# The hand-over from a window graph block to a two-way ConvLSTM scan: a new order of row blocks, and scan step 0 directly behind the last gather

## The reference, cut to what matters

```python
# layer 0: x is (16, 48, 32, 32)
y = affine(conv1x1(x, fc1_w, fc1_b), fc1_s, fc1_t)
nodes = windows of 8x8 pixels, 64 nodes of 48 channels each
idx = knn_idx(nodes, 9)                       # by normalized distance
feat = concat([x_i, x_j - x_i]); h = gelu(affine(feat @ ew + eb)); h = max over the 9 neighbours
x1 = affine(conv1x1(h, fc2_w, fc2_b), fc2_s, fc2_t) + x
...
# layer 1: rows of x1 are the time steps of a ConvLSTM, forward and backward
def step(carry, xr):                          # xr: (B, C, W), one image row
    h, c = carry
    gates = conv1d(concat([xr, h]), w_mid, width 3) + b
    i, f, g, o = split(gates, 4)
    c2 = sigmoid(f) * c + sigmoid(i) * tanh(g)
    h2 = sigmoid(o) * tanh(c2)
    return (h2, c2), h2
hs_f = scan(step, x1 rows 0..31); hs_b = scan(step, x1 rows 31..0)
y = w_proj @ concat([hs_f, hs_b]); y = relu(batchnorm(y)) + x1
```

## Time and profile before

| | us |
|---|---|
| median of 3 runs | 713.08 (711.72 to 713.14) |
| profiled execution, own time | 711.41 |
| span of the profiled execution | 709.5 |
| PE / DVE / ACT / POOL busy | 594.8 / 547.1 / 469.0 / 121.0 |
| mean granted PE clock | 0.94 |

### The profile page before, as it was taken

The page is one execution under the profiler, slowest core; times in us unless marked ns, Lnnn a source line. Parts: engine busy times, 40 slices in busy tenths (PEclk is TensorE's granted clock), DMA queues, the critical chain, the costliest instruction groups (busy, mean ns, idle before and its releaser), DMA issues.

```text
span 709.5 us, 12789 instructions
## 1 busy us (share of the span) xinstructions
PE 594.8 (84%) x3380; PEld 340.0 (48%) x3380; DVE 547.1 (77%) x1035; ACT 469.0 (66%) x675; POOL 121.0 (17%) x106
## 2 busy tenths in 40 slices
PE   5966799999999999987847888888889999988930
PEld 1213555555555555544414555555555555545500
DVE  1678799999999999993883777777777778767745
ACT  3631488888888888883852666666666666756635
POOL 2620122222222222233546000000000000000000
PEclk9987799999999999996987999999999999999965
DMA  8847755655655656686312111111111222276216
GB/s 221 256 130 194 187 121 132 130 132 131 134 133 131 135 130 132 134 154 141 73 18 56 44 45 44 45 45 45 41 30 52 69 74 72 55 155 152 77 55 177
DMA packets 98621, 75.99 MB, mean 107 GB/s; under 512 B 51765, under 2 KB 80951, under 8 KB 97879
## 3 DMA queue, kind: packets, MB, share of 16 engines
q1 hardware_dynamic: 97830, 72.06, 43.6%
q10 hardware_dynamic: 768, 3.67, 2.1%
HBM read 48.74 MB, written 22.35 MB: 100 GB/s over the span
## 4 chain that ended last, share of the span: by engine, by line
PE 45%; ACT 17%; DVE 13%; issue 13%; DMA 7%; SPq 3%; ACTq 1%; DVEq 1%
PE pz L602 13%; PE pz L695 8%; PE pz L688 6%; PE p_out L610 4%; ACT he L882 3%; ACT tgo L873 3%; ACT gel L813 3%; DMA y_d<-y 3%; PE p_edge L563 3%; PE p_keys L550 2%; PE pz L674 2%; ACT selfg L807 2%; PE p_edge L565 2%; PE p_edge L706 2%; ACT tif L867 2%
## 5 line engine op out<-in xcount | busy, mean ns | idle before, releaser
L1140 DVE TENSOR_REDUCE hmax<-gel 96x128 f32<-96x1024 f32 x128 | 154.1, 1205 | 33.1 <-ACT gel L813 32.5
L813 ACT ACTIVATE gel<-pz 96x1024 f32<-96x1024 f32 x128 | 130.7, 1023 | 58.2 <-PE pz L602 56.7
L674 PE MATMUL pz<-xh,w_xh 128*112 (+1 forms) x384 | 102.9, 404 | 8.2 <-issue 8.2
L695 PE MATMUL pz<-ht,w_xh 128*112 128x512 f32 x384 | 107.1, 414 | 3.1 <-DMA ht<-xh 3.1
L877 ACT ACTIVATE tc<-c 48x512 f32<-48x512 f32 x64 | 40.2, 628 | 68.0 <-DVE c L1228 68.0
L674 PEld LDWEIGHTS pz<-xh,w_xh 128*112 128x112 f32 x384 | 68.0, 177 | 33.4 <-issue 9.5
L695 PEld LDWEIGHTS pz<-ht,w_xh 128*112 128x112 f32 x384 | 62.1, 175 | 44.0 <-issue 24.9
L1235 DVE SCALAR_TENSOR_TENSOR h<-tgo,tc 48x512 f32<-48x512 f32 x64 | 44.0, 688 | 49.3 <-ACT tc L877 49.3
L688 PE MATMUL pz<-ht,w_e 48*112 48x512 f32 x192 | 60.7, 423 | 23.6 <-ACT he L882 23.6
L1033 POOL TENSOR_TENSOR xh<-kl,xh 48x512 f32 (+1 forms) x32 | 38.6, 1208 | 175.3 <-DVE idx L1116 90.4
L1219 DVE SCALAR_TENSOR_TENSOR cu<-tif,c 48x512 f32<-48x512 f32 x64 | 44.1, 690 | 24.6 <-ACT tif L867 23.2
(11 more groups left out here) (114 smaller groups left out, 1021.3 us busy)
## 6 DMA issues: line engine op xcount, KB each, us to landing
ib<-idx_d SPq DMA_DIRECT2D x64, 256.0 KB, 4.4
y_d<-y SPq DMA_DIRECT2D x32, 192.0 KB, 3.4
y_hl<-y_d SPq DMA_DIRECT2D x32, 192.0 KB, 4.3
hist_d<-h SPq DMA_DIRECT2D x64, 96.0 KB, 1.9
hp<-hist_d SPq DMA_DIRECT2D x32, 192.0 KB, 2.7
kr<-xn_d SPq DMA_DIRECT2D x32, 98.0 KB
xn_d<-x_in SPq DMA_DIRECT2D x32, 96.0 KB, 2.2
kl<-xn_d SPq DMA_DIRECT2D x32, 96.0 KB
```

The costliest lines, as they stand in the source:

```text
L674: pe.matmul(pz[0:TOP, 2 * d + m, :], w_xh[:, 0, d, m, t], rhs, start=(t == 0), stop=False)
L695: mm = pe.matmul(pz[0:TOP, 2 * d + m, :], w_xh[:, 1, d, m, t], moving(ht, slice(0, P), t), start=False, stop=(t == TAPS - 1))
L813: act.activation(gel[:, t % 2], pz[0:O, 2 * (t % 2):2 * (t % 2) + 2, :], ACT.Gelu) \
L1140: dve.tensor_reduce(dst, gel[:, t % 2].rearrange("p w (r c k) -> p w r c k", r=WS, k=KN), AX_X, ALU.max).then_inc(S["maxed"], 1)
```

## The change

Row blocks are processed in order 0, 3, 2, 1, by a function `place` that turns a group number into row block and pair. After 16 groups the scan has the rows it needs for its first 8 steps in both directions. Scan step 0 waits on PE for `x1_split` 16, `wl_split` 2 and the gelu of the gather that used the same PSUM banks, and leaves out its L688 matmuls (h is zero). fc2 of the last group follows step 0 on PE, `fc2_out` and `x1_high` of it are placed inside ACT's steps 0 and 1, and step 1 waits for `wl_split` 3.

The scan weights are loaded two turns earlier, scaled by POOL one turn earlier, and split by DVE in turns 29, 30 and 31, in place of the `topk` calls that these turns don't have. The rests in the padding rows come out of a masked multiply-add (raw weight plus head times 0 or -1 per partition). The mask `rests` is set by a POOL memset, four transfers of one element per partition, and a POOL multiplication. The four transfers L390 and the tile `wl_rest` are gone. The padding rows of `x1r` are loaded by one more transfer per step 26 to 29, in place of POOL's memset. One more pair of turns (24, 25) is written out rather than looped.

```diff
-            wr, p = g // PAIRS, g % PAIRS
+            wr, p = place(g)
...
+        def place(g):
+            return g // PAIRS * 3 % WROWS, g % PAIRS
...
-            with engine.Fori(1, GROUPS // 2 - 3) as j:
+            with engine.Fori(1, GROUPS // 2 - 4) as j:
...
@@ SP, load_scan_weights @@
-                sp.wait_ge(S["wl_split"], 3)
-                for k, first, n in ((0, C, HALF - C), (0, TOP, P - TOP), (1, C + 1, 1), (1, TOP, P - TOP)):
-                    sp.dma_start(w_xh[first:first + n, k].bitcast(F32), wl_rest[...]).then_inc(S["wl_moved"], 16)
+                sp.wait_ge(S["rests_set"], 1)
+                for k, first, n in ((0, C, HALF - C), (0, TOP, P - TOP), (1, C + 1, HALF - C - 1), (1, TOP, P - TOP)):
+                    sp.dma_start(rests[first:first + n, k:k + 1], ones_sel[0:n, 0, 0:1],
+                                 allow_slow_non_contiguous=True).then_inc(S["rests_here"], 16)
...
@@ SP, turn @@
-                if isinstance(j, int) and nth(j, b, 0)[0] == GROUPS - 6:
+                if isinstance(j, int) and nth(j, b, 0)[0] == GROUPS - 8:
                     load_scan_weights()
-                if isinstance(j, int) and nth(j, b, 0)[0] == GROUPS - 2:
+                if isinstance(j, int) and nth(j, b, 0)[0] in (GROUPS - 4, GROUPS - 3):
+                    d = nth(j, b, 0)[0] - (GROUPS - 4)
+                    sp.wait_ge(S["x1_hi"], 2 * PAIRS)
+                    sp.wait_ge(S["pads_set"], 9)
                     for s in range(2):
-                        load_twins(s, 0, s)
-                    sp.wait_ge(S["pads_set"], 9)
-                    load_third(0, 0)
+                        load_twins(s, d, s)
+                    load_third(0, d)
...
@@ SP, behind the turns @@
-            move_scan_weights()
-            sp.wait_ge(S["x1_hi"], GROUPS)
-            (twins and third of direction 1; store_x1 of the last group; its waits; loads of wp, gb, comb)
             step(0, 0)
+            store_x1(GROUPS - 1, 1, GROUPS // 2 - 1)
+            step(1, 1)
+            (waits for all x1 stores and x1_split 32; loads of wp, gb, comb)
...
@@ SP, steps 26 to 29 @@
+                    sp.dma_start(x1r[C:HALF, reg(i, 0, 4)],
+                                 x1_d[reg(i, H // 2, 4), 0:HALF - C].rearrange("r c b w -> c r (b w)")) \
+                        .then_inc(S["x1r_loaded"], 16)
...
@@ PE @@
-            pe.wait_ge(S["gelus"], 4 * GROUPS)
-            pe.wait_ge(S["wl_split"], 4)
-            pe.wait_ge(S["wl_moved"], 64)
+            pe.wait_ge(S["x1_split"], 2 * PAIRS)
             pe.wait_ge(S["zeros_set"], 2)
+            pe.wait_ge(S["wl_split"], 2)
+            pe.wait_ge(S["gelus"], 4 * GROUPS - 1)
             x_part(0, 0, 0, 0)
             h_part(0, 0)
-            pe.wait_ge(S["x1_split"], GROUPS)
+            pe.wait_ge(S["gelus"], 4 * GROUPS)
             x_part(0, 1, 0, 0)
             h_part(0, 1)
             x_part(1, 0, 1, 0)
+            fc2(GROUPS - 1, 1, GROUPS // 2 - 1)
+            pe.wait_ge(S["wl_split"], 3)
...
@@ ACT, step @@
+                    if isinstance(s, int) and s == 0 and d == 1:
+                        fc2_out(GROUPS - 1, 1, GROUPS // 2 - 1)
                     tanh_cell(s, d)
                     if d == 0:
                         tanh_i_f(s, 1)
...
+                    if isinstance(s, int) and s == 1 and d == 0:
+                        x1_high(GROUPS - 1, 1, GROUPS // 2 - 1)
...
@@ POOL @@
-                if isinstance(j, int) and GROUPS - 5 <= nth(j, b, 0)[0] < GROUPS - 3:
+                if isinstance(j, int) and GROUPS - 6 <= nth(j, b, 0)[0] < GROUPS - 4:
...
-            pool.memset(x1r[32:HALF], 0.0).then_inc(S["x1r_pads"], 1)
...
@@ DVE, called behind each topk's place in turns 29 to 31 @@
+            def scan_weights(g, part):
+                if g == GROUPS - 3:
+                    if part == 0:
+                        dve.wait_ge(S["wl_scaled"], 9)
+                    dve.tensor_copy(wl_head[:, part], wl_raw[:, part]).then_inc(S["wl_heads"], 1)
+                elif g == GROUPS - 2:
+                    dve.wait_ge(S["wl_heads"], part + 1)
+                    dve.scalar_tensor_tensor(w_xh[:, part], wl_head[:, part].bitcast(F32), rests[:, part:part + 1],
+                                             wl_raw[:, part], ALU.mult, ALU.add).then_inc(S["wl_split"], 1)
+                elif part == 0:
+                    dve.tensor_copy(wl_head[:, 2], wl_raw[:, 2]).then_inc(S["wl_heads"], 1)
+                else:
+                    dve.wait_ge(S["wl_heads"], 3)
+                    dve.tensor_tensor(w_e[:], wl_raw[:, 2], wl_head[:, 2].bitcast(F32), ALU.subtract) \
+                        .then_inc(S["wl_split"], 1)
```

More of the change, by code:

```diff
@@ L324, in store_x1 @@
                 sp.wait_ge(S["x1_sum"], g + 1)
-                wr = g // PAIRS
-                p = g % PAIRS
+                wr, p = place(g)
                 for h in range(2):
@@ L466, in _ @@
             step(0, 0)
-            with sp.Fori(0, H // 4 - 2) as j:
+            store_x1(GROUPS - 1, 1, GROUPS // 2 - 1)
+            step(1, 1)
+            for b in range(2):
+                sp.wait_ge(S[f"x1_stored{b}"], 32 * (GROUPS // 2))
+            sp.wait_ge(S["x1_split"], GROUPS)
+            sp.dma_start(wp_sb[:], wp).then_inc(S["consts2"], 16)
+            sp.dma_start(gb_sb[:], gb).then_inc(S["consts2"], 16)
+            sp.dma_start(comb_sb[:], comb).then_inc(S["consts2"], 16)
+            with sp.Fori(1, H // 4 - 1) as j:
                 for b in range(2):
-                    s = j * 2 + (1 + b)
+                    s = j * 2 + b
                     for d in range(2):
                         load_third(s + 1, d)
-                        load_twins(s + 2, d, 1 - b)
+                        load_twins(s + 2, d, b)
                         store_h(s, d)
-            for s in range(13, 18):
+            for s in range(14, 18):
                 step(s, s % 2)
@@ L478, in _ @@
                     step(j * 2 + (18 + b), b)
-            sp.wait_ge(S["x1r_pads"], 1)
+            sp.wait_ge(S["wl_split"], 3)
             with sp.Fori(0, 2) as j:
@@ L657, in _ @@
             turns(pe, turn)
-            fc2(GROUPS - 1, 1, GROUPS // 2 - 1)
             def x_part(s, d, b, n=None):
@@ L683, in moving @@
                     return t[rows, d, k:k + (W + 1) * B].rearrange("p (b w) -> p b w", w=W + 1)[:, :, 0:W]
-                for t in range(TAPS):
-                    for m, src in ((0, ht), (1, he)):
-                        rows = slice(HALF * m, HALF * m + C)
-                        pe.matmul(pz[0:TOP, 2 * d + m, :], w_e[rows, d, m, t], moving(src, rows, t),
-                                  start=False, stop=False)
-                if later(s):
+                if later(s):
+                    for t in range(TAPS):
+                        for m, src in ((0, ht), (1, he)):
+                            rows = slice(HALF * m, HALF * m + C)
+                            pe.matmul(pz[0:TOP, 2 * d + m, :], w_e[rows, d, m, t], moving(src, rows, t),
+                                      start=False, stop=False)
                     pe.wait_ge(S["h_lo"], s * 2 + (d - 1))
@@ L857, in _ @@
             x1_high(GROUPS - 2, 0, GROUPS // 2 - 1)
-            fc2_out(GROUPS - 1, 1, GROUPS // 2 - 1)
-            x1_high(GROUPS - 1, 1, GROUPS // 2 - 1)
             def tanh_i_f(s, d):
@@ L913, in _ @@
             step(0, 0)
-            with act.Fori(0, H // 4) as j:
+            step(1, 1)
+            step(2, 0)
+            with act.Fori(1, H // 4) as j:
                 for b in range(2):
@@ L1004, in scan_state @@
                 pool.wait_ge(S["pads_set"], 9)
+                pool.memset(rests[:], 0.0).then_inc(S["rests_set"], 1)
             def scan_weights(part):
@@ L1163, in turn @@
                 on(3, topk, 0)
+                if not exists(nth(j, b, 3)[0]):
+                    scan_weights(now[0], 0)
                 maxima(*now, 1)
@@ L1166, in turn @@
                 on(3, topk, 1)
+                if not exists(nth(j, b, 3)[0]):
+                    scan_weights(now[0], 1)
                 maxima(*now, 2)
```

53 lines of the change are left out of this document (16 added, 37 removed).

## The result

The changed kernel takes 701.88 us, the median of 4 runs (700.95 to 702.55), against 712.4 for the kernel before (709.91 to 713.14: the three runs shown and one beside the changed kernel). The ratio is 0.9858, with a 95% interval of 0.9829 to 0.9886: about 10 us faster, where 7.9 were forecast (705.2 as the median). The profiled execution went from 711.41 to 701.45, the span from 709.5 to 699.5. The page of the changed kernel shows where not to look: the engines do the same work, 5 us less of it on POOL and 7 us more on DVE than in the earlier trace rows.

A forecast was written before the change was run, and what follows sets the result against it. Neither PE (84% busy) nor DVE (77%) alone set the time; stages were read singly. Gains and losses, 11.6 - 0.5 - 1.0 - 2.2 = 7.9 us, took 711.4 to 703.5; the median, 1.7 above, was 705.2, range 698.5 to 710.

The forecast's parts named there:

- Hand-over: From turn 29 to the scan's first cu: cu comes 13.0 us earlier, bounds 11.0 and 14.6.
- The yardstick: DVE's first cu in the scan, at 383.30 in the kernel before: how much earlier it comes.
- Three signs: Turn 30 longer by 1.4 to 2.4, self_max of turn 31 ending near 370 (old scale), clock 1.00 throughout the hand-over.
- if all idle is filled, DVE is done at 370.2: DVE in turns 29 to 31: 20.19 us of work plus 6.93 added from 343.10; 372.3 if half the idle stays.
- Steps 0 and 1: First scan steps: 0.4 gained without L688 matmuls, 0.6 lost to x1_high, 1.2 lost to POOL beside DVE.
- the 1.2 for POOL: Scan's first steps: POOL's residual and x1_low of the last group slow DVE's cells; 1.2 us lost, bounds nothing and 2.47.
- Weights: Loading two turns earlier: stall moves to turn 25 unchanged; 0.5 us lost to later load_y, 1.0 to POOL's scaling.
- The tail: Scan steps 26 to 29: a sixth transfer ahead of load_third costs 2.2 us, bounds nothing and 3.6.
- The whole gain: Rival: idle filled, no POOL and DVE collision in the scan, transfers hidden; 14.4 us gained, 698.7; chance 0.14.
- A new wait at `x1_high` in step 1: Rival: ACT holds its queue until POOL's sum is through, 5.25 at worst; 708 to 711.5, chance 0.16.
- No change: Rival: SP's loads of twins and thirds in steps 0 to 3 were as late as PE's start; 713, chance 0.04.
- Slower by address arithmetic: Rival: place adds register work in 22 looped turns; at 0.5 us a turn the time is 716; chance 0.06.

The follow-up runs named there:

- the second trace of the kernel before: the kernel before run once more, unchanged, for its spread: 714.41 us.
- the serial kernel: changed kernel with step 0 again waiting for fc2, fc2_out, residual, x1_high and x1_low of the last group: 713.42 us, ratio 1.0049 to the kernel before.
- the second trace: the changed kernel run once more, unchanged: 702.3 us, ratio 0.9852 to the kernel before.
- the first combination: changed kernel with later fc2 of group 30, spread x1r rows, weights three a turn over turns 22 to 25: 690.33 us, ratio 0.9656 to the kernel before.

## Why the prediction was right in direction and small in size

**Hand-over, 13.0 forecast, 10.6 measured.** The yardstick was the right one, and DVE does set `cu`: `self_max` of turn 31 ends at 369.60 in the changed kernel. The 10.6 lies just below the bounds of 11.0 to 14.6. Three signs that it named did not come: turn 30 is longer by 11.22 - 7.97 = 3.3, not 1.4 to 2.4, `self_max` of turn 31 ends at 372.6 on the old scale, not near 370, and the clock is not 1.00. The step that failed is "if all idle is filled, DVE is done at 370.2", with its reason that "ACT and PE have slack in those turns". The forecast had 20.19 + 6.93 = 27.12 us of DVE work and no idle time. Measured are 8.45 + 11.12 + 8.48 = 28.05 of work, 0.9 more, and 29.57 - 28.05 = 1.5 of idle time. The multiply-add was well priced (1.61 for 1.54). Of the 0.9, 0.75 stands in turn 30 (11.12 against 7.29 + 3.08 = 10.37): there DVE met POOL, a collision that the sum had only inside the scan. The 1.5 is a loop that was not followed: DVE late with the maxima holds up gelus and fc2(30), PE stops for 4.08 and returns at a lower clock, and DVE later waits for the gelus of turn 31. PE reached `x_part` 365.17 - 340.06 = 25.1 us after the start of turn 29, where 365.4 - 343.10 = 22.3 was the forecast. The experiment with fc2(30) moved confirms the loop (2.15 back). That with the multiply-adds spread fits the collision: turn 30 is 2.3 shorter, 0.8 for a copy in place of a multiply-add and 1.5 for the two stretched instructions that are not there. It does not show that POOL was out of the way, since POOL ran beside both; it had not started first.

**Steps 0 and 1, a loss of 1.4 forecast, 0.3 measured** (from `cu` of step 0 to that of step 2, 17.38 before, 17.65 after; the second trace of the kernel before, with its lower clock, has 18.88). Step 0 is 0.4 shorter (8.06 after 8.42), as forecast for the left-out matmuls, and step 1 is 0.6 longer (9.59 after 8.96), as forecast for `x1_high`; the serial kernel, with neither `x1_high` nor POOL in the scan, has 8.08 and 8.86. So of the 1.2 for POOL hardly 0.1 is to be seen. `residual` and `x1_low` of group 31 took 1.28 and 1.19, and each met one DVE instruction, as DVE's timeline of the changed kernel shows:

```profile
376.56 1.07 DVE L1249 SCALAR_TENSOR_TENSOR h<-tgo,tc 48x512 f32<-48x512 f32 x1 [0.69 <-ACT tc L878]
...
383.41 1.13 DVE L1223 TENSOR_TENSOR ht<-h,ht 48x512 fp32r<-48x512 f32 x1 [0.63 <-ACT ht L889]
```

They took 0.4 longer each than the 0.69 they take alone. The 2.5 us of passes could cost the scan so little because a pass meets DVE only where the two overlap, and DVE idles between its cells. By the rule of the Trainium skill (GPSIMD Engine Reference, "Key points"), POOL contends with instructions of two SBUF inputs. Both rows agree with it, and so does the 2.63 of turn 30. The collision belonged in the sum, but for turn 30.

**Weights, 1.5 forecast, nothing to be seen.** The stall keeps its size within the scatter whichever turn it is in: turns 24 to 29 take 63.70 and 63.66 in the kernel before, and 62.12 to 64.57 after. The four transfers of masks took 3.00 us of SP's queue (2.2 in the second trace), more than the 2.0 allowed for, and no loss from them is to be seen, which fits the reason given then (`load_y` lands when the backlog has drained). In the changed kernel's SP timeline:

```profile
289.18 4.91 SPq L388 DMA_DIRECT2D wl_raw<-wl  x11
294.14 3.00 SPq L391 DMA_DIRECT2D rests<-ones_sel  x4
297.19 0.42 SPq L290 DMA_DIRECT2D y_hl<-y_d  x1
```

In the chain of waits the last of them lands 7.22 us later, where it was 11.77 in the earlier trace rows:

```profile
297.19 7.22 DMA y_hl<-y_d
```

What the issue takes longer the landing takes less, and more than that: 4.6 less for 3.0 more here, 2.5 less for 2.2 more in the second traces (8.84 after 11.37). The scaling beside DVE in turns 26 and 27 took longer itself (the first part 5.68 against 3.97 in the earlier trace rows), but the turns little (9.12 and 8.90 against 8.64), and turn 28 is 1.1 shorter (9.29 after 10.39).

**The tail, 2.2 forecast, 2.7 measured** as the mean of seven traces with the sixth transfer (43.28) over two of the kernel before (40.61). Mechanism and size hold; the scatter is as large as the effect, 41.97 to 45.18 over the seven.

**The rivals.** The whole gain: no, the hand-over stayed 4.0 short of its bound of 14.6, and the tail took 2.7. A new wait at `x1_high` in step 1: the sum took 1.28, not 5.25. In the kernel before it had started inside the first of two subtractions and waited for both: they end at 374.13, 1.2 more is 375.3, and it ended at 375.26. In the scan no DVE instruction is that long. No change: no, SP's twins and thirds were in place. Slower by address arithmetic: the looped turns take 8.64 in the mean, after 8.62 in both traces of the kernel before, some 0.4 us over the whole loop. The median lies 3.3 below the forecast. By the table, hand-over and tail gave 2.4 and 1.2 less than forecast, steps 0 to 25 gave 0.9 more, turns 24 to 28 gave 3.4 more (1.5 of a loss that is not there, 1.9 of scatter), start and rest 1.4 more (scatter again): 2.1 in all. The rest is that this profiled execution stands 0.4 below its median, where that of before stood 1.7 below. So the median is nearer to the forecast than its terms are: two of them erred in opposite directions, and the scatter helped, which is luck. The second pair of traces divides its 13.3 otherwise: 11.3 in the hand-over, nothing in turns 24 to 29, 1.1 in steps 0 to 25 (the slower step 0 of the kernel before), a tail that costs 1.5, and 2.4 in start and rest.

## What to carry to other kernels

Before work is moved off a path, look at what else ends there: the splits lay next to a chain on other engines, and a kernel with the splits moved and both directions made to wait for that chain had a hand-over of 32.12, no shorter than the 32.30 before. An experiment that puts an old order back must put back the old waits one by one; here one wait too many makes the share of the splits unreadable. A step that is taken out has to be looked for in every stretch that it stood in: the left-out L688 matmuls count in direction 0 too. Work that is put into the turns ahead has to fit turn by turn, not in the sum over the turns: here one turn that DVE overfilled stopped PE for 4.08 us, with a lower granted clock behind it. Many transfers put at one place in a queue cost little each and 3 to 10 us together; spread over earlier turns or steps they cost little or nothing here (turns 22 and 23 of the first combination 8.56 and 8.57, steps 18 to 25 with two more transfers each 75.59 after 75.73).

## What the runs showed of the hardware that was not expected

- POOL beside DVE: the one that starts later waits for the other. In eight cases a DVE instruction started while a two-input pass of POOL ran, and each ended 0.13 to 0.19 us before POOL's end plus its own time alone: the multiply-add (2.63 for 1.61), `self_max` of turn 31 (1.48 for 0.69), the two of the scan and the `one_hot` of turn 30 in the changed kernel, `c` of the kernel with the later fc2 (1.67), and the `one_hot` and the head copy (1.50 and 1.94) of the one with the spread multiply-adds. Where DVE started first it kept its time and POOL took up to 2.69 for 1.2. The maxima's reductions kept theirs either way (1.21 at 351.93, inside the 2.69 of `x1_low`). POOL's memset of 32 x 8192, 6.93 us and without inputs, stretched nothing (steps of 9.56 and 8.96 after 9.59 and 8.94).
- The low clock after the idle time at the hand-over lasted differently in two executions of the kernel before: 1.00 again by 382 in one, 0.50 until 386 in the other, 2.1 us of difference up to step 2. In the changed kernel both traces agree.
- Five or six transfers of x1r ahead of `load_third` differ by 2.7 us over four steps; two a step, eight steps earlier, cost none.
- The start of the kernel scatters by 4.3 us between traces (284.71 to 289.06), more than most parts of this change are worth. It is there already at `self_max` of group 2 (103.28 to 107.49). Its cause stays open, as does the exact reason for turn 29 of 10.02 in the kernel with the spread multiply-adds, seen once.
